# A macaron layer on eight cores: the first weight loads reordered, and the output pass with whole-tile matmul loops and the transposes ahead of the output projection

## What is computed

```python
x = x + 0.5 * (layernorm(x) @ sign(W).T)
h = layernorm(x)
Q = elu(h @ Wq.T + bq) + 1;  K = elu(h @ Wk.T + bk) + 1;  V = h @ Wv.T + bv   # 16 heads of 64
KV = sum_n K_n^T V_n;  Z = sum_n K_n                                           # over one sequence
x = x + ((Q @ KV) / (Q . Z + 1e-6)) @ Wo.T + bo
x = x + 0.5 * (layernorm(x) @ sign(W).T)
```

## Time and profile before

| | |
|---|---|
| time, median of 3 runs | 2119.31 us (2117.68 to 2119.91) |
| the profiled execution's own time | 2119.46 us |
| its span on the slowest core (core 5) | 2117.8 us |
| spans of all cores | 2105.9 to 2117.8 us |
| TensorE matmul busy | 1771.5 us (84%) |
| TensorE weight loads busy | 790.9 us (37%) |
| ScalarE busy | 1227.4 us (58%) |
| VectorE busy | 771.3 us (36%) |
| start of the first matmul | 70.38 us |

### The profile page before, as it was taken

How to read it: one execution, slowest core, us unless ns; L and a number is a source line. 1 busy time by engine, 2 the same in 40 slices (tenths; PEclk the granted TensorE clock), 3 DMA queues, 4 the chain that set the end, 5 groups by cost and what they waited for, 6 DMA issues and landing times.

```text
span 2117.8 us, 33127 instructions; the slowest of 8 cores (2105.9 to 2117.8 us)
## 1 busy us (share of the span) xinstructions
PE 1771.5 (84%) x10784; PEld 790.9 (37%) x10784; DVE 771.3 (36%) x2113; ACT 1227.4 (58%) x2025; POOL 147.5 (7%) x274
## 2 busy tenths in 40 slices
PE   0499899899889989889989989688888888888887
PEld 0233333333333333333333333344444444444443
DVE  2133333333333333333333332243434344444443
ACT  1367767766766776776776776444444444444443
POOL 1000000000000010000000000001010101010100
PEclk9999999999999999999999999899999999999999
DMA  8622222222222232222222221132323333333332
GB/s 175 123 78 76 87 89 66 87 88 72 82 87 85 70 115 91 65 87 74 80 87 88 67 87 59 50 125 100 125 102 123 102 124 105 120 109 116 109 116 75
DMA packets 134631, 199.35 MB, mean 94 GB/s; under 512 B 88384, under 2 KB 88384, under 8 KB 134464
## 3 DMA queue, kind: packets, MB, share of 16 engines
q0 software_dynamic: 32960, 109.08, 15.8%
q1 hardware_dynamic: 101504, 88.15, 13.7%
HBM read 104.87 MB, written 83.89 MB: 89 GB/s over the span
## 4 chain that ended last, share of the span: by engine, by line
PE 53%; ACT 27%; issue 13%; DMA 3%; DVE 2%; ACTq 1%; DVEq 0%; SPq 0%
PE pA L470 22%; PE pA L481 12%; PE pA L602 11%; ACT u1b L449 4%; ACT mnb L404 3%; ACT mxb L406 3%; PE pA L485 2%; PE pA L605 2%; ACT nb L364 2%; ACT eb L405 2%; ACT kbQ L392 2%; ACT u2fm L442 2%; PE tpB L460 2%; ACT attnfm L436 2%; PE pA L475 2%
## 5 line engine op out<-in xcount | busy, mean ns | idle before, releaser
L481 PE MATMUL pA<-wv,u1fm 128*128 128x512 bf16 x1024 | 245.5, 383 | 96.7 <-ACT kbK L408 96.7
L602 PE MATMUL pA<-wo,attnfm 128*128 128x512 bf16 x1024 | 244.8, 382 | 84.4 <-ACT attnfm L438 84.4
L578 PE MATMUL pA<-sw,u2fm 128*128 128x512 bf16 x1024 | 232.9, 380 | 56.6 <-ACT u2fm L444 54.4
L481 PE MATMUL pA<-wk,u1fm 128*128 128x512 bf16 x1024 | 242.4, 379 | 18.3 <-ACT kbQ L392 18.3
L470 PE MATMUL pA<-sw,u0fm 128*128 128x512 bf16 x1024 | 236.6, 385 | 0.0
L470 PE MATMUL pA<-wq,u1fm 128*128 128x512 bf16 x1024 | 232.1, 380 | 0.0
L442 ACT COPY u2fm<-tpB 128x512 bf16<-128x512 bf16 x64 | 37.5, 586 | 333.4 <-PE tpB L460 333.4
L481 PEld LDWEIGHTS pA<-wv,u1fm 128*128 128x128 bf16 x1024 | 91.0, 98 | 213.3 <-issue 123.8
L314 DVE TENSOR_TENSOR phiQ<-eb,mxb 128x1024 bf16<-128x1024 bf16 x64 | 44.3, 692 | 344.1 <-ACT mxb L406 344.1
L348 DVE SCALAR_TENSOR_TENSOR y2t<-pA,y1in 128x1024 f32<-128x1024 f32 x64 | 78.4, 1224 | 249.4 <-PE pA L605 249.4
L389 ACT ACTIVATE u2b<-y1t 128x1024 bf16<-128x1024 f32 x63 | 66.6, 1057 | 176.3 <-DVE y1t L283 176.2
(11 more groups left out here) (121 smaller groups left out, 2475.6 us busy)
## 6 DMA issues: line engine op xcount, KB each, us to landing
xt<-x SPq DMA_DIRECT2D x64, 512.0 KB, 3.9
y1scr<-y1t POOLq DMA_DIRECT2D x64, 512.0 KB, 3.9
y1in<-y1scr POOLq DMA_DIRECT2D x64, 512.0 KB, 4.2
out<-y3t SPq DMA_DIRECT2D x64, 512.0 KB, 2.6
qscr<-qfm POOLq DMA_DIRECT2D x64, 256.0 KB, 3.2
qfin<-qscr POOLq DMA_DIRECT2D x64, 256.0 KB, 4.3
qfm<-phiQ SPq DMA_TRANSPOSE x512, 2.3
stg<-wfT SPq DMA_DIRECT2D x4, 512.0 KB, 8.5
```

The lines of the kernel that those rows point to most:

```text
L481: mm = e.matmul(dst[:, h*512:(h+1)*512], lhs_fm[:, c*P:(c+1)*P], w_sb[:, c, h*512:(h+1)*512], start=(c == 0), stop=(last and c == 7))
L578: mm = e.matmul(pA2[:, h*512:(h+1)*512], u2fm[:, (t - 3) % 2, c*P:(c+1)*P], sw[:, c, h*512:(h+1)*512], start=(c == 0), stop=(c == 7))
L602: e.matmul(pA2[:, h*512:(h+1)*512], attnfm[:, (t - 1) % 2, c*P:(c+1)*P], wo[:, c, h*512:(h+1)*512], start=(c == 0), stop=False)
```

## The change

Two separate places.

**Startup.** SP issues the first four chunks of `wfT` ahead of the four x tiles. They go round six buffers and no longer two: `stg`, both of `y3t`, `y2t[:, 1]`, both of `y1in`. Each load still waits for the one before to land; the wait for ScalarE stays only for the last two chunks.

**Output pass.** FFN 2 and the output projection use `proj` in its `cw` form: chunks outside, halves inside, one count at the end, and a start on the first half of the input. VectorE evicts FFN 2 in one operation of 1024 columns instead of two of 512, `vY3` counts tiles, and the output projection waits for the whole eviction. The transposes of `u2b` (step 4) now stand ahead of the output projection (step 3). The programs of ScalarE and POOL keep their order.

```diff
--- before.py
+++ after.py
@@ -156,16 +156,20 @@
 
         @block.sync
         def _(e):
+            stg_bufs = [stg[:, 0, :], y3t[:, 0, :], y3t[:, 1, :], y2t[:, 1, :],
+                        y1in[:, 0, :], y1in[:, 1, :]]
+            for c in (0, 1, 2, 3):
+                if c >= 1:
+                    e.wait_ge(gStg, 16 * c)
+                e.dma_start(out=stg_bufs[c], in_=wfT[c*P:(c+1)*P, :]).then_inc(gStg, 16)
             for t0 in range(4):
                 s, j = t0 // NJ, t0 % NJ
                 e.dma_start(out=xt[:, t0 % 4, :], in_=x[s, j*P:(j+1)*P, :]).then_inc(dIn[t0 % 4], 16)
-            for c in range(8):
-                buf = stg[:, 0, :] if c % 2 == 0 else y3t[:, 0, :]
-                if c >= 2:
-                    e.wait_ge(sSw, c - 1)
-                if c >= 1:
-                    e.wait_ge(gStg, 16 * c)
-                e.dma_start(out=buf, in_=wfT[c*P:(c+1)*P, :]).then_inc(gStg, 16)
+            for c in (4, 5, 6, 7):
+                if c >= 6:
+                    e.wait_ge(sSw, c - 5)
+                e.wait_ge(gStg, 16 * c)
+                e.dma_start(out=stg_bufs[c % 6], in_=wfT[c*P:(c+1)*P, :]).then_inc(gStg, 16)
             for t in range(NT):
                 if t + 4 < NT:
                     tl = t + 4
@@ -184,7 +188,7 @@
                                 transpose=True).then_inc(dQT, 16)
             for t in range(NT):
                 s, j = t // NJ, t % NJ
-                e.wait_ge(vY3, 2 * (t + 1))
+                e.wait_ge(vY3, t + 1)
                 if t >= 2:
                     e.wait_ge(dY3o[t % 2], 16 * (t // 2))
                 e.dma_start(out=out[s, j*P:(j+1)*P, :], in_=y3t[:, t % 2, :]).then_inc(dY3o[t % 2], 16)
@@ -317,15 +321,10 @@
             for t in range(NT + 3):
                 if 3 <= t <= NT + 2:
                     tf = t - 3
-                    v.wait_ge(tFfn2, 2 * t - 5)
+                    v.wait_ge(tFfn2, t - 2)
                     if tf >= 2:
                         v.wait_ge(dY3o[tf % 2], 16 * (tf // 2))
-                    v.scalar_tensor_tensor(y3t[:, tf % 2, 0:512], pA2[:, 0:512], 0.5,
-                                           y2t[:, tf % 2, 0:512],
-                                           ALU.mult, ALU.add).then_inc(vY3, 1)
-                    v.wait_ge(tFfn2, 2 * t - 4)
-                    v.scalar_tensor_tensor(y3t[:, tf % 2, 512:1024], pA2[:, 512:1024], 0.5,
-                                           y2t[:, tf % 2, 512:1024],
+                    v.scalar_tensor_tensor(y3t[:, tf % 2, :], pA2[:, :], 0.5, y2t[:, tf % 2, :],
                                            ALU.mult, ALU.add).then_inc(vY3, 1)
                 if t < NT:
                     v.wait_ge(tNum, t + 1)
@@ -340,7 +339,7 @@
                 if 1 <= t <= NT:
                     tw = t - 1
                     if 3 <= t <= NT + 2:
-                        v.wait_ge(vY3, 2 * (t - 2))
+                        v.wait_ge(vY3, t - 2)
                     v.wait_ge(tWo, t)
                     v.wait_ge(dY1i[tw % 2], 16 * (tw // 2 + 1))
                     if t >= 3:
@@ -366,9 +365,11 @@
 
         @block.scalar
         def _(e):
+            sgn_bufs = [stg[:, 0, :], y3t[:, 0, :], y3t[:, 1, :], y2t[:, 1, :],
+                        y1in[:, 0, :], y1in[:, 1, :]]
             for c in range(8):
                 e.wait_ge(gStg, 16 * (c + 1))
-                e.sign(sw[:, c, :], stg[:, 0, :] if c % 2 == 0 else y3t[:, 0, :]).then_inc(sSw, 1)
+                e.sign(sw[:, c, :], sgn_bufs[c % 6]).then_inc(sSw, 1)
             for t0 in (0, 1, 2):
                 e.wait_ge(vVr1, t0 + 1)
                 ln_apply(e, ssync, vr1, t0, negm1, r01, nb1, sR01, t0 + 1)
@@ -571,15 +572,9 @@
                 if 3 <= t <= NT + 2:
                     e.wait_ge(vY2, min(t - 1, NT))
                     if t > NT:
-                        e.wait_ge(vY3, 2 * (t - 3))
-                    e.wait_ge(sU2fm, 2 * t - 4)
-                    for h in range(2):
-                        for c in range(8):
-                            mm = e.matmul(pA2[:, h*512:(h+1)*512],
-                                          u2fm[:, (t - 3) % 2, c*P:(c+1)*P],
-                                          sw[:, c, h*512:(h+1)*512], start=(c == 0),
-                                          stop=(c == 7))
-                        mm.then_inc(tFfn2, 1)
+                        e.wait_ge(vY3, t - 3)
+                    proj(e, u2fm[:, (t - 3) % 2, :], sw, pA2[:, :], None, tFfn2,
+                         cw=(sU2fm, 2 * t - 5))
                 if t < NT:
                     s = t // NJ
                     p2 = t % 2
@@ -593,23 +588,16 @@
                         mm = e.matmul(pden[:, 2*c:2*c+2], qfin[:, p2, c*P:(c+1)*P], zexp[:, s, c, :],
                                       start=True, stop=True)
                     mm.then_inc(tNum, 1)
-                if 1 <= t <= NT:
-                    e.wait_ge(sAttnfm, 2 * t)
-                    for h in range(2):
-                        if t >= 3:
-                            e.wait_ge(vY3, 2 * t - 5 + h)
-                        for c in range(8):
-                            e.matmul(pA2[:, h*512:(h+1)*512],
-                                     attnfm[:, (t - 1) % 2, c*P:(c+1)*P],
-                                     wo[:, c, h*512:(h+1)*512], start=(c == 0), stop=False)
-                        mm = e.matmul(pA2[:, h*512:(h+1)*512], ones_row[0:1, :],
-                                      bor[0:1, h*512:(h+1)*512], start=False, stop=True)
-                    mm.then_inc(tWo, 1)
                 if 2 <= t <= NT + 1:
                     e.wait_ge(sU2, t - 1)
                     if t >= 3:
                         e.wait_ge(sU2fm, 2 * t - 4)
                     transposes8(e, u2b[:, (t - 2) % 2, :], tpB, tU2T)
+                if 1 <= t <= NT:
+                    if t >= 3:
+                        e.wait_ge(vY3, t - 2)
+                    proj(e, attnfm[:, (t - 1) % 2, :], wo, pA2[:, :], bor, tWo,
+                         cw=(sAttnfm, 2 * t - 1))
                 if t < NT:
                     e.wait_ge(vAttn, t + 1)
                     if t >= 1:
```

## The result

The changed kernel takes 2079.5 us (median of 10 runs) against 2119.1 before: the ratio is 0.9806, 95% interval 0.9796 to 0.9817, or 41 us less. Some executions, of either kernel, are slower at a lower granted clock on one die or both; the ratio leaves them out and the median doesn't, so the two differ a little. The forecast was 2072, the range 2060 to 2090. The profiled execution took 2075.97 us with a span of 2074.3.

A forecast was written before the change was run, and what follows sets the result against it. Bounds: a startup chain of transfers one at a time, and an output-pass loop over three engines, not TensorE. From 2119.46, 41.7 us for the output pass and 6 for the startup gave 2072; range 2060 to 2090.

The forecast's parts named there:

- Projection to `y2t`: Output pass, first section of the period: one change less to the one-row bias saves 0.21 us, 4.60 to 4.39.
- `y2t` to the projection: Output pass, second section of the period: the last of three chains sets it, 7.07 us becomes 6.62.
- Chain c): Output pass, from `y2t` through FFN 2 and its one-piece eviction to the next projection: ends last, 6.62 us, up to 6.69.
- The release: Output pass, TensorE's wait after FFN 2's eviction: taken as 0.18 us, between 0.15 and 0.25.
- a): Output pass, from `y2t` through squares, `u2b` and the moved transposes to the next projection: 6.56 us.
- b): Output pass, from `y2t` through squares and the first half of `attnfm` to the next projection: 6.58 us.
- The number of periods: Output pass, tile 2 to tile 63: 61 periods, each 0.66 us shorter, 40.3 us in all.
- Startup, 6 us: Startup: fifth chunk lands at 35 us, the last three one at a time until 61 instead of 67.1, 6 us less.
- The spread of the cores before: Kernel before: cores differ by 12 us because core 5 gets its eighth chunk later than core 6, with the same work afterwards.
- The eviction as the bound: Rival, output pass: FFN 2 released no earlier than +1.62, period 11.22, 35 us less, 2085; chance 0.13 for 2080 to 2088.
- The x tiles in the way: Rival, startup: each train transfer about 8.9 us, eighth chunk at 88, total 2099; late startup up to 2100 has chance 0.10.
- The clock: Rival, output pass: halves inside drop TensorE to its lower clock level, 3.3 us a period, +200, 2272 us; chance 0.03.

The follow-up runs named there:

- the run with late weights: Full change, but POOL issues the four attention weights only when all eight chunks have landed; ratio 0.9784 to the kernel before.
- the kernel with the train: Full change, but no chunk waits for the one before to land, each with its own semaphore; ratio 0.9713 to the kernel before.
- the transposes back: Full change with the transposes of `u2b` back behind the output projection; ratio 0.9788 to the kernel before.
- the kernel with halves: Full change, but FFN 2 with halves outside and its eviction in two halves as before; ratio 0.9757 to the kernel before.

## Why the prediction was right, point by point

**Projection to `y2t`, 4.60 to 4.39.** Shown: 4.39 (1705.06 to 1709.45); alone it gave 0.19 a period, where 0.21 was reckoned.

**`y2t` to the projection, 6.62.** It is 6.75 (1709.45 to 1716.20). Chain c) ended last, as forecast, and its terms were short by little: FFN 2 after `y2t` 1.49 (1.49), FFN 2 to eviction 3.79 (3.72), eviction and release 1.47 (1.41). The release, which I set at 0.18 between bounds of 0.15 and 0.25, was 0.24. Chains a) and b) were real too. With FFN 2 in halves and the transposes moved, a) ends last, at 6.53 (1705.83 to 1712.36; reckoned 6.56); with them in their old place b) does, at 6.49 (1706.44 to 1712.93; reckoned 6.58). The mean periods, 10.96 and 10.92, lie at the 10.97 that 4.39 + 6.58 makes.

**The number of periods.** I reckoned each of the 61 with the gain of a typical one: 40.3 us. They gave 30.8. The typical period lost 0.53, not 0.66, by the 0.13 that chain c) was longer: 7.9 us. The other 1.6 are above all one period of 12.83 us at a lowered clock (last section). This is the term that was mis-sized, by 9.5 us.

**Startup, 6 us.** The sum for a core with early weights was right (fifth chunk 35.4 for 35, last sign 61.5 for 61; the train of five took 17.5 us, for 3.3 each and 1 more). That POOL's weights start at 14.5 us was right for one core of eight. Shown by the run with late weights: what a chunk costs depends on whether they have started. That the time followed this sum is in part luck: in the profile the one core with early weights was the slowest, and the edit alone gained 12 us (8 to 16), not 6.

**What the sum left out.** The output pass gave 32.8 us where 41.7 were forecast (30.8 in the periods, 2 around its ends for 1.4). That the total missed by 4 to 7 us and not by 9 is owed to 5.2 us that stood in no term: the 1.8 of the first tiles, and 3.4 because core 1 escaped two falls of the clock in the first pass that core 5 had before. The second is luck.

**The spread of the cores before.** I put the 12 us between cores 5 and 6 down to the startup, with the same work afterwards. The startup holds 5.8 of them (first matmul at 70.4 and 64.6 us). The first pass holds 4.7 more, most of it in the same two periods at a lowered clock, and the end of the output pass 1.6.

**The rivals.** The eviction as the bound, 11.22: nearly so, by another way; FFN 2 did start at +1.49, and the loop closed over the eviction all the same. The x tiles in the way: not so, five transfers took 17.5 us. The clock: it does fall in this loop, but in one period of 61, on seven of the eight cores, and again in the last FFN 2, as before.

**What the prediction named as the gain.** It put the loop order, the half start, the moved transposes and the earlier FFN 2 into one sum. The experiments part them: half start 0.60 us a period, the projection's loop order 0.19, moved transposes 0, and FFN 2's new loop with its eviction in one piece costs 0.25 of it again. Of the four edits of the output pass, the rewritten projection alone gains; the other three could have stayed out.

## What to carry to other kernels

Where a matmul waits for an operand that another engine copies in pieces, start it on the first piece with the contraction outside; before merging an eviction into one instruction, look at what waits for its last column. A chain of small transfers, each waiting for the one before, pays the queue's delay each time when a bulk load runs beside it: put them in flight together, or before the bulk load, and look at what else stands behind the bulk load in its queue. When one core sets the time, look at all of them: a race between two queues may fall differently on each.

## What the runs showed of the hardware that I had not expected

The period of 12.83 us in the full change is a fall of TensorE's clock. In the windows of core 1, whose third column from the right is the granted clock, it is 0.61 and 0.54 where its neighbours have 1.00, towards the lower of its two levels (1.2 and 2.4 GHz):

```profile
1830.00:1834.00 4.00, 2.62 (x18) 1.05 (x15) 1.23 (x2) 0.01 (x1) 0.00 (x0) 1.00 0.01 2
1834.00:1836.00 2.00, 1.85 (x5) 0.68 (x6) 0.47 (x5) 1.15 (x2) 1.07 (x2) 0.61 0.27 33
1836.00:1838.00 2.00, 2.00 (x7) 0.76 (x6) 0.13 (x1) 1.45 (x4) 0.00 (x0) 0.54 0.86 291
1838.00:1840.00 2.00, 2.00 (x25) 1.29 (x24) 0.37 (x1) 1.45 (x3) 0.00 (x0) 1.00 0.20 78
```

```profile
1834.15 5.30 PE L471 MATMUL pA<-sw,u2fm 128*128 128x512 bf16 x16 [1.53 <-DVE y2t L347]
```

Before it TensorE had idled 1.53 us, where a typical period has 1.18. FFN 2 then took 5.30 us instead of 3.61. The same period is stretched on every core of the full change but core 4, and on six of eight in the kernel with the train; it is on no core of the kernels with the transposes back or with halves. The kernel with nothing but the transposes moved has two such periods, 12.32 us each, on six of its eight cores: again FFN 2 takes 5.30 us, after 1.55 and 1.53 us of idle, and there its halves are outside. So in these runs the falls inside the loop come with the moved transposes, which leave TensorE idle for longer between the projection and FFN 2, and not with the order of the halves. But the idle alone doesn't decide it. Core 4 has the same 1.53 us in the same period, and its FFN 2 takes 3.61:

```profile
1828.04 3.61 PE L471 MATMUL pA<-sw,u2fm 128*128 128x512 bf16 x16 [1.53 <-DVE y2t L347]
```

Near the start of the pass every core of the full change has an idle of 1.53 us or more too, without a fall, and the kernel with halves has 1.53 twice without one. Two periods of the first pass have the like on some cores and not on others: 21.5 us instead of 19.9 each, on six cores before the change and five after it. They make most of the 3.4 us that core 1 is ahead of core 5 in the first pass. The Trainium skill, TensorE: Matmul & The Clock Gate, A second HAM failure mode: psum-queue depth-cycling, tells of such swings for matmuls that cycle through PSUM banks; here the form with the halves inside runs at the upper level in 60 or 61 of the 61 periods, depending on the core, and with the transposes moved alone the form with the halves outside had more falls, so these traces don't show its rule at work. What decides on which core and in which period the clock falls stays open; no run here was made to find out.

A store took 46.9 us from issue to landing behind the weight loads of its own queue, against a median of 3.9 us over all 64 stores of the full change.
